# Graph attention on one core: seven of 416 edge tiles copied row by row by SyncE and ScalarE instead of gathered by GpSimd

## What is computed

```
h = (x @ W).reshape(n, HEADS, OUT_DIM)                # 8 heads of 32
a_src = einsum('nhc,hc->nh', h, att_src);  a_dst = einsum('nhc,hc->nh', h, att_dst)
e = leaky_relu(a_src[src] + a_dst[dst], 0.2)
m = segment_max(e, dst);  e = exp(e - m[dst]);  denom = segment_sum(e, dst)
out = segment_sum(h[src] * (e / (denom[dst] + 1e-16))[:, :, None], dst)
```

## Time and profile before

| | us |
|---|---|
| runs, median of 3 | 2845.5 |
| runs, lowest and highest | 2841.72 and 2847.04 |
| the profiled execution, its own time | 2839.73 |
| its span in the trace | 2837.6 |
| first gather of the attention stage issued at | 2085.8 |
| last gather issued at | 2715.8 |

### The profile page before, as it was taken

One profiled execution on the slowest core, in us unless ns is written; L12 is line 12 of the kernel. 1 busy time (PEld: TensorE's weight loads), 2 busy tenths in 40 slices (PEclk: granted clock), 3 DMA queues, 4 the chain that ended last, 5 costly groups with the idle time before them and its releaser, 6 DMA issues.

```text
span 2837.6 us, 31034 instructions
## 1 busy us (share of the span) xinstructions
PE 2222.4 (78%) x8708; PEld 1505.3 (53%) x8708; DVE 1482.2 (52%) x4063; ACT 662.7 (23%) x1371; POOL 1215.7 (43%) x1733
## 2 busy tenths in 40 slices
PE   3777898999989999999999999999923535354450
PEld 2444798446766555655556555677712424233340
DVE  7999876556870010440005302455536757575668
ACT  3777655114540010200001000355400000000002
POOL 0000488888888700010000000000158888888860
PEclk9898899999999999999999999999966666666675
DMA  8565698443445444464345434433343333333321
GB/s 295 223 247 238 209 291 283 151 148 98 140 122 192 117 153 152 149 209 154 128 154 182 156 116 127 111 97 103 88 87 94 97 94 98 95 97 95 94 77 45
DMA packets 191911, 411.95 MB, mean 145 GB/s; under 512 B 47734, under 2 KB 131409, under 8 KB 191761
## 3 DMA queue, kind: packets, MB, share of 16 engines
q1 hardware_dynamic: 124676, 237.38, 26.3%
q10 hardware_dynamic: 30925, 105.42, 10.3%
q0 software_dynamic: 36160, 67.34, 9.0%
HBM read 326.06 MB, written 83.96 MB: 144 GB/s over the span
## 4 chain that ended last, share of the span: by engine, by line
PE 54%; POOL 19%; DVE 17%; issue 5%; DMA 3%; ACT 2%; ACTq 0%; SPq 0%; DVEq 0%; POOLq 0%
PE banks L1519 25%; POOL row_ring L2154 10%; PE banks L942 8%; DVE features_and_rows L568 6%; POOL spare_count L339 5%; POOL table_dense_weights L792 3%; PE banks L2377 3%; PE banks L1186 3%; PE banks L1201 3%; PE banks L1069 3%; DVE pair_and_bias_rows L565 2%; PE banks L1506 2%; PE banks L1962 1%; PE banks L1489 1%; PE banks L1979 1%
## 5 line engine op out<-in xcount | busy, mean ns | idle before, releaser
L792 POOL DMA_INDIRECT table_dense_weights<-pair_weight,dst x416 | 416.6, 1001 | 390.1 <-DVE weights_c L837 315.0
L1519 PE MATMUL banks<-own_term,features_and_rows 128*128 128x391 f32 (+1 forms) x1656 | 554.1, 492 | 6.7 <-DMA own_term<-table_dense_weights 6.7
L2154 POOL DMA_INDIRECT row_ring<-table_heads,src x416 | 408.9, 983 | 67.4 <-issue 65.3
L1519 PEld LDWEIGHTS banks<-own_term,features_and_rows 128*128 128x128 f32 x1656 | 312.9, 190 | 234.6 <-issue 8.8
L1545 DVE TENSOR_SCALAR features_and_rows<-banks,hop_bias 128x391 f32<-128x391 f32 (+1 forms) x24 | 15.0, 625 | 615.1 <-PE banks L1519 615.1
L942 PE MATMUL banks<-split_rows,count_columns 128*128 128x512 f32 x1200 | 310.7, 406 | 3.2 <-ACT count_columns L924 2.4
L1519 PE MATMUL banks<-features_and_rows 128*128 128x391 f32 (+1 forms) x840 | 282.4, 491 | 0.0
L339 POOL IOTA spare_count<- 128x256 int32 x728 | 263.7, 362 | 7.2
L2377 PE MATMUL banks<-row_ring,edge_to_window 128*128 x880 | 238.1, 435 | 17.0 <-DVE edge_to_window L2352 13.4
L942 PEld LDWEIGHTS banks<-split_rows,count_columns 128*128 128x128 f32 x1200 | 222.4, 189 | 52.7 <-issue 5.3
L1627 POOL DMA_INDIRECT hidden<-table_counts,edge_weight x12 | 11.3, 938 | 552.6 <-DVE edge_weight L1636 343.0
(11 more groups left out here) (423 smaller groups left out, 2959.1 us busy)
## 6 DMA issues: line engine op xcount, KB each, us to landing
hidden<-table_counts SPq DMA_DIRECT2D x305, 160.0 KB
table_dense_weights<-weights_c ACTq DMA_DIRECT2D x26, 1600.0 KB, 5.7
own_term<-table_dense_weights SPq DMA_DIRECT2D x52, 782.0 KB
own_term<-table_dense_weights SPq DMA_DIRECT2D x34, 780.5 KB
pair_and_bias_rows<-table_edge_rows ACTq DMA_DIRECT2D x50, 512.0 KB
weights_c<-table_edge_rows ACTq DMA_DIRECT2D x50, 512.0 KB
features_and_rows<-table_dense_weights SPq DMA_DIRECT2D x26, 782.0 KB
table_counts<-hidden SPq DMA_DIRECT2D x25, 800.0 KB, 3.5
```

The source lines that it names most:

```text
L792: e.indirect_dma_start(out=self.table, out_offset=bass.IndirectOffsetOnAxis(ap=self.place[:, t:t + 1], axis=0), in_=self.values[:, t:t + 1 ...
L1519: m = e.matmul(psum[b][:, 0:wide], z_block(block)[:, f * P:(f + 1) * P], streamed[tile % STREAM][:, lo - from_column:lo - from_column + wi ...
L2154: e.indirect_dma_start(out=ring_rows[:, ring_at(t), 0:ATT_ROW], out_offset=None, in_=t_h, in_offset=bass.IndirectOffsetOnAxis(ap=src[:, t: ...
```

## The change

Tiles 63, 127, 191, 255, 319 and 383 (the last tile of every second part) are fetched by SyncE's queue and tile 62 by ScalarE's. For each, 128 DMAs of one row; the row's number is read from a small tile `source_rows` into a register, 16 registers at a time, and the DMA's source address comes from the register. GpSimd leaves these tiles out, with their pauses. Each of the seven tiles has a semaphore of its own, and the weighing of its part waits for it too.

Tile 62 and tile 63 are issued as soon as the table is written and the row numbers have landed; SyncE's other five wait for `merged` of the tile 80 before them.

```diff
+SYNC_TILES = {b: (b + 1) * PART_TILES - 1 for b in range(1, PARTS, 2)}
+SCALAR_TILE = 2 * PART_TILES - 2
+ROW_TILES = (*SYNC_TILES.values(), SCALAR_TILE)
+ROW_REGS = 16
...
+        s_tile_rows = {t: pr.sem(f"tile_rows_landed{t}") for t in ROW_TILES}
+        s_row_src = pr.sem("source_rows_loaded")
+        pr.queue["sp"].append(lambda e: [e.dma_start(row_src[n:n + 1, :], a["src_run"][0:1, 1 + t * P:1 + (t + 1) * P]).then_inc(s_row_src, 16)
+                                         for n, t in enumerate(ROW_TILES)])
+
+        def load_tile_rows(e, t, regs):
+            n = ROW_TILES.index(t)
+            for p in range(P):
+                if p % ROW_REGS == 0:
+                    e.load(regs, row_src[n:n + 1, p:p + ROW_REGS])
+                node = e.snap(regs[p % ROW_REGS], min_val=0, max_val=PADDED_NODES - 1)
+                e.dma_start(ring_rows[p:p + 1, ring_at(t), 0:ATT_ROW], t_h[bass.ds(node, 1), :]).then_inc(s_tile_rows[t], 16)
...
-                for t in range(quad * GROUP, (quad + 1) * GROUP):
+                for t in tiles_of(quad):
+                    if t in ROW_TILES:
+                        continue
                     e.indirect_dma_start(out=ring_rows[:, ring_at(t), 0:ATT_ROW], out_offset=None, in_=t_h,
...
+            row_regs = [e.alloc_register(f"source_row{k}") for k in range(ROW_REGS)]
+            e.wait_ge(*w_h)
+            e.wait_ge(s_row_src, 16 * len(ROW_TILES))
+            load_tile_rows(e, SYNC_TILES[1], row_regs)
             for b in range(2, PARTS):
                 e.wait_ge(*cuts_read[b - 2])
                 load_start_cut(e, b)
+                if b in SYNC_TILES:
+                    if SYNC_TILES[b] >= RING_TILES:
+                        e.wait_ge(*merged(SYNC_TILES[b] - RING_TILES))
+                    load_tile_rows(e, SYNC_TILES[b], row_regs)
...
             landed = [row_landed(quad) for quad in part_quads(b)]
+            landed += [(s_tile_rows[t], 16 * P) for t in ROW_TILES if t // PART_TILES == b]
...
         def merge_act(e):
+            row_regs = [e.alloc_register(f"scalar_source_row{k}") for k in range(ROW_REGS)]
+            e.wait_ge(*w_h)
+            e.wait_ge(s_row_src, 16 * len(ROW_TILES))
+            load_tile_rows(e, SCALAR_TILE, row_regs)
```

More of the change, by code:

```diff
@@ L211, in residual_gnn @@
         node_of = sb("node_of_tail_row", [P, 2], I32)
+        row_src = sb("source_rows", [P, P], I32)
         row_head = sb("head_of_row", [P, 1])
@@ L2110, in residual_gnn @@
         s_row = [pr.sem(f"edge_rows_landed{k}") for k in range(RING_QUADS)]
-        row_landed = lambda quad: (s_row[quad % RING_QUADS], 16 * GROUP * (quad // RING_QUADS + 1))
+        tiles_of = lambda quad: range(quad * GROUP, (quad + 1) * GROUP)
+        gathered = lambda quad: sum(t not in ROW_TILES for q in range(quad % RING_QUADS, quad + 1, RING_QUADS) for t in tiles_of(q))
+        row_landed = lambda quad: (s_row[quad % RING_QUADS], 16 * gathered(quad))
+        s_tile_rows = {t: pr.sem(f"tile_rows_landed{t}") for t in ROW_TILES}
[9 more added lines that the diff above has]
+                e.dma_start(ring_rows[p:p + 1, ring_at(t), 0:ATT_ROW], t_h[bass.ds(node, 1), :]).then_inc(s_tile_rows[t], 16)
         part_quads = lambda b: range(b * PART_TILES // GROUP, (b + 1) * PART_TILES // GROUP)
```

## The result

The changed kernel is slower: median 2977.63 us of four runs (2967.76 to 2978.49) against 2846.03 of four runs of the kernel before, a ratio of 1.0458 with an interval of 1.0433 to 1.0482. The profiled execution took 2978.2 us with a span of 2976.0, 138.5 us more than that of the kernel before.

A forecast was written before the change was run, and what follows sets the result against it. GpSimd's gathers were taken as the bound, SyncE's late rows as the new pace: 640c - 174.5, with c = 0.52 us a row, adds 158.3 to 2839.7 us, plus 5.8 for the median: 3004 us, range 2945 to 3110.

The forecast's parts named there:

- The bound: Attention stage: GpSimd's gathers set the pace, 1.518 us a tile; seven left out make 10.6 us if rows arrive in time.
- The place that decides: SyncE's wait for tile 127's slot: released at the eighth step of part 2's merge, 6.4 us after it begins.
- GpSimd's stop: GpSimd, before tile 152's gather: stands until 4.0 us after part 3's late merge begins; idles some 25 to 35 us.
- One sign of being wrong: Profile after the change: the prediction would be wrong if GpSimd stayed busy at 89%.
- A row (c): SyncE's cost of one row: issue, gaps, address and register load, 0.52 us together, 66.6 us a tile.
- The landing: Rows on SyncE: a tile is complete about 128c + 2.3 us after SyncE's release, c being a row's cost.
- The pace: Parts 3 to 11: SyncE, not GpSimd, sets the pace, odd parts' merges 128.7 us apart.
- The sum: Merge starts: part 3's at 2342.9, part 11's at 2857.7, part 12's copies at 2877.7; profiled execution 158.3 us longer.
- What was costed at nothing: Stage's side effects: late tile 63, ScalarE's tile 62, row-number loads, one more VectorE wait a part, delayed start cuts: no cost.
- the queue did not fill: Rival on SyncE's queue: it fills up, a row costs 1.17 us, time 3420 us; chance 0.05.
- no row waited for the landing of another: Rival on SyncE's queue: rows do not overlap, a row costs 2.8 us, time about 4460 us; chance 0.02.
- the wait is not that of the tile's own merge: Rival on SyncE's wait: only the tile's own merge, window some 70 us, rows fit; chance within the 0.04 for a gain.

The follow-up runs named there:

- first_tile: Changed kernel with SyncE taking the first tile of every second part instead of the last: 2833.01 us against 2846.1 before the change; run again, 2837.85 against 2848.2.
- one_dma: Changed kernel with each of the seven tiles fetched by one DMA of table rows 0 to 127, edges' own rows left out: 2836.05 us against 2846.1 before the change.
- more2: Against `more`: 12 tiles, all first of their parts, tile 62 back with GpSimd, ScalarE's tiles placed earlier between its moves: 2827.67 us against 2848.2 before the change.
- tile22: Changed kernel with SyncE taking the 23rd tile (32b + 22) of every second part instead of the last: 2852.0 us against 2845.57 before the change, ratio 1.0027.
- tile24: Changed kernel with SyncE taking tile 32b + 24 of every second part instead of the last: 2955.35 us against 2845.57 before the change, ratio 1.0382.
- two_alone: Changed kernel keeping only tiles 62 and 63 as row DMAs, the other five gathered by GpSimd again: 2843.06 us against 2844.97 before the change, ratio 0.999.
- more: Changed kernel with SyncE on odd parts' first tiles and ScalarE on tile 62 and even parts' first tiles, 13 in all: 2881.27 us against 2844.97 before the change.

## Why the prediction was right

The forecast was 3004 us, slower, with a range of 2945 to 3110; 2977.63 lies inside, 26.4 us under the likeliest value. Step by step:

- **The bound.** GpSimd's gathers set the pace, 1.52 us each. `first_tile`, `one_dma` and `more2` gave back about that for each tile left out, 1.4 to 1.9 us by their medians.
- **The place that decides.** The eighth step of part 2's merge was read out of a count and out of the earlier trace rows, and it stands: the first row follows the start of that merge by 7.8 us in part 2 and 7.1 in part 4, 1.2 of them for the load of its number, where the release was forecast at 6.4. `tile22` and `tile24` show the step between two merges directly.
- **GpSimd's stop.** The gather of tile 152 starts 4.3 us after part 3's late merge begins (2344.10 to 2348.36), where 4.0 was forecast. One sign of being wrong, GpSimd busy at 89%, does show in the window up to 2300; that window lies ahead of the first stop, and behind it the share is 69%.
- **A row (c).** Here a term was mis-sized, in two directions. I took 0.32 us for the issue, "since fewer destinations should shorten it and the register should lengthen it"; it takes 0.225, less than the shortest of the earlier trace rows, and less than the 0.253 of the one-row loads with a fixed address, so no lengthening by the register shows. A MOVE of 0.029 and a third gap were not counted, and the load of 16 registers takes 1.23, not 1.10. Together 0.496 instead of 0.52: release and rows take 71.0 us for tile 127 (2256.04 to 2327.04) and 70.4 for tile 191 instead of 73.0.
- **The landing.** I took 2.3 us from the end of the last row's issue to its use, out of a small transfer's 2.8; 1.1 was measured (2327.04 to 2328.12).
- **From part to part.** Copies to merge 16.0 instead of 16.7, odd to even merge 36.2 instead of 36.7.
- **The pace.** 36.2 + 70.4 + 1.1 + 16.0 = 123.7 for parts 3 to 5, where I had 128.7; over four pairs 123.2. Before it was 96.2; the prediction's 96.7 is twice the distance of parts 2 and 3.
- **The sum.** Part 3's merge was forecast at 2342.9 and came at 2344.1: 3.9 us were saved by the terms above, while part 2's merge stood 5.1 us later than I had put it (2256.04, not 2250.95), mostly since the stage began 4.5 us later, at 2090.3. Four pairs at 5.5 us less put part 11's merge at 2836.8 instead of 2857.7, and part 12's copies at 2858.0 instead of 2877.7. The shift of the profiled executions is 138.5, not 158.3; that of the medians 131.6. Why the stage began later is not shown; in every other trace here its first gather stands later than the 2085.8 before, too (2088.0 to 2093.6). For the median I had added 5.8 us, by which the profiled execution before lay under the median. If the later start is the same difference, the 26.4 us by which the median was missed are nearly the terms alone, 3.9 + 4 x 5.5 = 25.9.

What was costed at nothing held, once with luck. Tile 63 delays part 1's copies a little (2194.2, forecast 2192.8), and the gain or loss of `two_alone` is too small to tell. The start cut behind tile 127 is issued at 2327.09, before VectorE even begins the part. ScalarE's tile 62 was forecast to be through by about 2175. ScalarE's issues by source line and its first move say otherwise:

```profile
L2130 ACTq DMA_DIRECT2D row_ring<-table_heads x128: 234/234/541, 2126.5 to 2189.4; - x128
...
2191.78 0.18 ACT L2422 ACTIVATE weights_c<-banks 128x8 f32<-128x8 f32 x1 [103.28 <-issue]
```

Its rows begin only at 2126.5, some 19 us after the seven loads of row numbers were issued, where I had counted on their landing soon after their issue. It costs nothing because tile 63's rows end later still, at 2192.5. So the first move is held back from 2167.91 to 2191.78, and `two_alone`, which keeps this, loses nothing. GpSimd's stops of about 28.6 us lie inside the 25 to 35 that were forecast.

The rivals: the queue did not fill (no issue over 0.37 us on SyncE), no row waited for the landing of another, and the wait is not that of the tile's own merge. The Trainium skill (DMA: Bandwidth & Descriptors, section "Issuing engines are not separate DMA queues") calls the time to start a DMA usually small beside the DMA. For rows of 1 KB the trace of the changed kernel shows it otherwise: SyncE issues for 63.23 us, and the last row is there 1.1 us later, while as many bytes as one DMA took an issue of 0.32.

What stays open: `merged` allows 25 steps for borders between node tiles, and a wait for the tile's own step should release SyncE earlier with the last tile too. That wait was not tried, since it would hold for one list of edges only. The 2.3 us by which `more2` gained more than its gathers, and the 2.7 us between the two runs of `first_tile`, are not explained either; they are near what runs of this kernel differ by.

## What to carry to other kernels

If a slower engine helps to fill a ring, give it the item whose slot is released first, and work out from the wait's real count, not from its name, how long it has until the item is wanted: here the same 63 us of issuing a tile gain 10 to 13 us in all with the first tiles of the parts and lose 132 with the last ones. Count the instructions that one transfer takes on its issuing engine before the bytes, and look for what stands ahead of them in that engine's list (`more` lost by a move ahead of tile 384's rows and by tile 62 ahead of tile 64's). A loss by a missed deadline comes back in every round of the ring, since the late merge releases the next slot late too.

## What was not expected of the hardware

- A DMA of one row with its address in a register is issued in 0.225 us on SyncE and 0.234 on ScalarE, quicker than any DMA of this queue before (0.256 for 53 rows), and quicker than a one-row DMA of 512 bytes with a fixed address (0.253 on SyncE).
- 128 rows in a row are complete 1.1 us after the last issue ends, 1.3 after it begins, although a small transfer by itself took 2.8 us from the start of its issue to landing.
- 896 such rows, of 1056 bytes, beside 416 gathers changed neither the gathers (1.521 us against 1.518) nor the time (1.0003).
